# Degrees of the first graph: a search in the sorted destinations in place of a one-hot histogram, and the edge loads inside the first stage

## What is computed

```python
xn = _layernorm(x)
x = x + gnn(xn, (src, dst), w1, b1, gamma, beta, w2, b2, w_gcn, b_gcn) + mix(xn)
x = x + ffn(_layernorm(x), edge_index, ...)

def gnn(x, edge_index, ...):
    h = x @ w1.T + b1
    h = relu((h - mean(h, 0)) * rsqrt(var(h, 0) + eps) * gamma + beta)
    xw = (h @ w2.T + b2) @ w_gcn.T
    # src, dst get one loop edge per node
    deg = segment_sum(ones, dst, n)
    dinv = rsqrt(max(deg, 1))
    return segment_sum(xw[src] * (dinv[src] * dinv[dst])[:, None], dst, n) + b_gcn
```

## Time and profile before

| | |
|---|---|
| median of three executions | 5221.02 us |
| span of the profiled execution | 6013.1 us |
| instructions | 46816 |
| TensorE matmul busy | 4326.3 us (72%) |
| VectorE busy | 2806.5 us (47%) |
| GpSimd busy | 2975.4 us (49%) |
| ScalarE busy | 805.6 us (13%) |

### The profile page before, as it was taken

How to read it: one execution, slowest core, us unless ns; L and a number is a source line. 1 busy time by engine, 2 the same in 40 slices (tenths; PEclk the granted TensorE clock), 3 DMA queues, 4 the chain that set the end, 5 groups by cost and what they waited for, 6 DMA issues and landing times. The chain is left out here.

```text
span 6013.1 us, 46816 instructions
## 1 busy us (share of the span) xinstructions
PE 4326.3 (72%) x14757; PEld 2849.2 (47%) x14757; DVE 2806.5 (47%) x6018; ACT 805.6 (13%) x1519; POOL 2975.4 (49%) x2919
## 2 busy tenths in 40 slices
PE   5999777778779888778886545778687777630077
PEld 3776644444445555555554533445454444420045
DVE  5777466565556545666664621222222222232066
ACT  1111511222200000000000110112121111110022
POOL 0000266666666556677776024555545554466600
PEclk8666888888877788777777556888888888765589
DMA  3110533333344455333336552232223232232078
GB/s 102 48 53 30 145 112 112 113 112 113 107 113 132 141 137 144 91 90 90 90 90 79 177 147 50 81 89 84 69 74 88 83 87 80 60 85 54 11 180 220
DMA packets 257510, 596.30 MB, mean 99 GB/s; under 512 B 86189, under 2 KB 142304, under 8 KB 251903
## 3 DMA queue, kind: packets, MB, share of 16 engines
q0 software_dynamic: 119696, 294.84, 18.8%
q1 hardware_dynamic: 137582, 298.62, 17.9%
HBM read 437.77 MB, written 155.48 MB: 99 GB/s over the span
## 5 line engine op out<-in xcount | busy, mean ns | idle before, releaser
L941 POOL DMA_INDIRECT g_rows<-table,gcn_srcT x1664 | 1770.3, 1064 | 799.3 <-issue 472.8
L1804 POOL DMA_INDIRECT n_rows<-gtab,so_own x1122 | 1092.0, 973 | 885.2 <-DVEq L1923 551.2
L1011 PE MATMUL g_ps<-g_rows,g_hot 128*125 128x256 f32 x3328 | 1103.4, 472 | 225.5 <-issue 169.0
L1296 DVE TENSOR_TENSOR acc<-acc,g_ps 125x256 f32 x1664 | 697.3, 419 | 927.7 <-PE g_ps L1011 508.0
L1011 PEld LDWEIGHTS g_ps<-g_rows,g_hot 128*125 128x125 f32 x3328 | 723.1, 233 | 507.0 <-issue 342.9
L1750 PE MATMUL p_py<-f_w,f_hh 128*125 128x256 f32 x2688 | 678.8, 402 | 265.4 <-issue 261.9
L1744 PE MATMUL p_ph<-f_xfT,f_w 128*128 128x500 f32 x1344 | 627.7, 618 | 256.2 <-ACT f_hh L1975 128.5
L1750 PEld LDWEIGHTS p_py<-f_w,f_hh 128*125 128x125 f32 x2688 | 533.6, 199 | 426.8 <-issue 352.8
L1947 DVE TENSOR_TENSOR p_ob<-p_py,p_xb 125x512 f32<-125x512 f32 x168 | 114.7, 690 | 1299.9 <-remote 793.0
L1744 PEld LDWEIGHTS p_ph<-f_xfT,f_w 128*128 128x128 f32 x1344 | 268.8, 201 | 580.5 <-issue 433.2
L471 PE MATMUL a_pdeg<-so_x 125*100 125x125 bf16 x1600 | 372.5, 407 | 41.2 <-DVE so_x L552 41.2
(11 more groups left out here) (330 smaller groups left out, 4373.4 us busy)
## 6 DMA issues: line engine op xcount, KB each, us to landing
o_d<-p_ob SPq DMA_DIRECT2D x21, 1920.0 KB
z_ob<-o_d SPq DMA_DIRECT2D x21, 1920.0 KB
g_rows<-table,gcn_srcT POOLq DMA_INDIRECT x1664
n_rows<-gtab,so_own POOLq DMA_INDIRECT x1122
gout<-n_o SPq DMA_DIRECT2D x33, 408.0 KB
xnT_d<-a_xnT SPq DMA_DIRECT2D x25, 500.0 KB, 2.9
m_area<-xnT_d SPq DMA_DIRECT2D x25, 500.0 KB
qT_d<-m_area SPq DMA_DIRECT2D x25, 500.0 KB
```

Source lines behind the costliest of these rows:

```text
L941: pool.indirect_dma_start(out=rows[:, g % RING, j], out_offset=None, in_=K.table, in_offset=bass.IndirectOffsetOnAxis(ap=K.gcn_srcT[:, 4 * ...
L1011: mm = pe.matmul(ps[q, p % 4, b], hot[:, g % 4, 2 * j + b], rows[:, g % RING, 2 * j + b], start=True, stop=True, skip_group_check=True)
L1296: dve.tensor_tensor(a, a, ps[q, p % 4, b], ALU.add).then_inc(add_s, 1)
L1804: pool.indirect_dma_start(out=rows[:, c % 3, j], out_offset=None, in_=K.gtab, in_offset=bass.IndirectOffsetOnAxis(ap=K.gat_src[:, c * W + ...
```

## The change

The one-hot comparisons and the 1600 products are gone from `first_half`. For every tile t and partition p the kernel now finds how many edges have a destination below node 125 t + p, in two steps, and takes differences of neighbours for the degrees (126 partitions are used, so that each has its successor):

- The sorted destinations are written as 16-bit numbers into a DRAM table `gcn_dst` of 500 rows of 400. Every row's first value is spread over all partitions once (`phead`, 126x500 in PSUM, one product).
- Step one, `outside`, on VectorE: four comparisons per block of `phead` with the node number, each summed over its 500 columns. `choose` turns the counts into row numbers.
- GpSimd gathers those rows, four gathers of 126 rows of 800 bytes per block of nodes, into one of three buffers.
- Step two, `inside`, on ScalarE, three blocks later: four `Sign` activations of 126x400, each summed over its columns.
- Two small products at the end make degrees of the differences.

`load_edges` no longer exists. Its loads, the pair table, its write and the order check stand inside `first_half`, spread over the first blocks. What it did for unsorted edges alone moves behind the branch on the flag, in `places` and a new `degrees_unsorted`; so three branched stages now stand between `first_half` and `table_rows`, where two stood between `load_edges` and `first_half`.

```diff
-def load_edges(nc, m, K, A):
...
+def degrees_unsorted(nc, K):
...
+SPAN = 400
+HEADS = E_GCN // SPAN
+OWN = GCN_C // SPAN
+POST = TN + 1
...
             @block.sync
...
+                by_part = A.dst.rearrange("(p c) -> p c", p=c)
+                rows_in_two(sp, raw[:, 1], by_part, dst_s)
                 load(0)
                 for t, a in ((w1T, A.w1T), (w2, A.w2), (wgT, A.wgT)):
                     sp.dma_start(t[:], a.rearrange("(c p) o -> p c o", p=P)).then_inc(w_s, 16)
...
+                sp.wait_ge(short_s, 1)
+                rows_in_two(sp, K.gcn_dst.rearrange("(p i) h -> p (i h)", p=c), short, rows_out)
                 load(1)
                 load(2)
+                rows_in_two(sp, raw[:, 0], A.src.rearrange("(p c) -> p c", p=c), src_s)
 
                 sp.wait_ge(blank_s, 1)
...
+                    if k == 3:
+                        sp.wait_ge(pay_s, 2)
+                        rows_in_two(sp, K.gcn_pairs[0:E_GCN].rearrange("(p c) a -> p c a", p=c), K.gcn_pay, pairs_out)
...
+            @block.gpsimd
+            def _(pool):
...
+                pool.wait_ge(rows_out, 32)
+                for g in range(NB):
+                    pool.wait_ge(row_s, g + 1)
+                    if g >= DEEP:
+                        pool.wait_ge(side_s, 4 * (g - DEEP + 1))
+                    for j in range(4):
+                        pool.indirect_dma_start(out=rows[z, g % DEEP, j], out_offset=None, in_=K.gcn_dst,
+                                                in_offset=bass.IndirectOffsetOnAxis(ap=row[z, 4 * g + j:4 * g + j + 1], axis=0)
+                                                ).then_inc(got[g % DEEP], 16)
 
             @block.tensor
...
                 for k in range(NB):
-                    degrees(k * each)
+                    turn(k)
                     if k == 0:
                         pe.wait_ge(w_s, 16 * 5)
-                    turn(k)
-                    degrees(k * each + 1)
-                    degrees(k * each + 2)
                     project(k)
-                    degrees(k * each + 3)
...
+                pe.wait_ge(diff_s, 4)
+                pe.matmul(pdeg[q, 1, 0:NT], diff[z, 1], row_f[z], start=True, stop=False)
+                pe.matmul(pdeg[q, 1, 0:NT], diff[z, 0], inner[z], start=False, stop=True).then_inc(both_s, 1)
...
             @block.scalar
...
+                def inside(g):
+                    act.wait_ge(got[g % DEEP], 64 * (g // DEEP + 1))
...
+                    for j in range(4):
+                        t = 4 * g + j
+                        act.activation(seen[z, j], rows[z, g % DEEP, j], ACT.Sign, bias=minus[z, t:t + 1],
+                                       accum_out=side[z, t:t + 1]).then_inc(side_s, 1)
...
+                    if k in (1, 2):
+                        paired(2 - k)
+                    if k >= 3:
+                        inside(k - 3)
...
+                for g in range(NB - 3, NB):
+                    inside(g)
...
             @block.vector
...
+                def outside(g):
...
+                    for j in range(4):
+                        t = 4 * g + j
+                        dve.tensor_scalar(met[z, j], phead[z], node[z, t:t + 1], None, ALU.is_lt, ALU.add,
+                                          accum_out=heads[z, t:t + 1]).then_inc(met_s, 1)
...
                 for k in range(NB):
-                    if k:
-                        onehot(k * each)
                     if k + 1 < NB:
                         statistics(k + 1)
-                    onehot(k * each + 1)
+                    outside(k)
                     if k + 1 < NB:
                         normalise(k + 1)
-                    onehot(k * each + 2)
+                    choose(k)
                     if k:
                         of_h(k - 1)
-                    onehot(k * each + 3)
+                    check_order(k)
```

More of the change, by code:

```diff
@@ L305, in _ @@
                     scatter.run(pool, 0, GCN_C // ROUND)
-def load_edges(nc, m, K, A):
[L312 to L315, removed]
+def degrees_unsorted(nc, K):
+    HB = 16
+    rounds = GCN_C // HB
+    c = GCN_P
     with ExitStack() as ctx:
         m = Mem(nc, ctx)
[L319 to L330, removed]
-        with nc.Block() as block:
[L332 to L337, removed]
-                sp.wait_ge(copied, 2)
-                sp.dma_start(K.gcn_pairs[0:E_GCN].rearrange("(p c) a -> p c a", p=c), K.gcn_pay[0:c]).then_inc(out_s, 16)
-                sp.wait_ge(pad, 1)
-                sp.dma_start(K.gcn_pairs[E_GCN:E_GCN + P], tail[:]).then_inc(out_s, 16)
-                sp.wait_ge(out_s, 32)
-            @block.gpsimd
-            def _(pool):
-                pool.memset(tail[:, 0:1], 0).then_inc(chain, 1)
-                pool.memset(tail[:, 1:2], -1).then_inc(chain, 1)
-                pool.wait_ge(chain, 2)
-                pool.sem_inc(pad, 1)
@@ new lines, in degrees_unsorted @@
+        number = m.sb("du_number", [P, TN, HB], BF16)
+        on = m.sb("du_on", [P, TN, HB], BF16)
+        ot = m.sb("du_ot", [P, HB, NT], BF16)
+        blank = m.sb("du_blank", [P, P], BF16)
+        by_tile = m.sb("du_by_tile", [P, TN])
+        deg = m.sb("du_deg", [P, NT])
+        psum = m.ps("du_psum", [P, TN])
+        pturn = m.ps("du_pturn", [P, NT])
+        node_s, tile_s, used, numbered, deg_s, both_s, root_s = (m.sem("du_" + s) for s in (
+            "node", "tile", "used", "numbered", "deg", "both", "root"))
@@ L449, in _ @@
                         sp.dma_start(t[:], a.rearrange("(c p) -> p c", p=P)).then_inc(w_s, 16)
+                with nc.allow_non_contiguous_dma(reason="one value per partition"):
+                    sp.dma_start(after[0:c - 1], by_part[1:c, 0:1]).then_inc(after_s, 16)
+                sp.wait_ge(short_s, 1)
+                rows_in_two(sp, K.gcn_dst.rearrange("(p i) h -> p (i h)", p=c), short, rows_out)
                 load(1)
                 load(2)
+                rows_in_two(sp, raw[:, 0], A.src.rearrange("(p c) -> p c", p=c), src_s)
                 sp.wait_ge(blank_s, 1)
```

235 lines of the change are left out of this document (161 added, 74 removed).

## The result

| | before | after |
|---|---|---|
| median | 5220.52 us (5213.09 to 5234.57) | 4903.05 us (4898.74 to 4919.78), four executions |
| ratio | | 0.939, 95% interval 0.9368 to 0.9412 |
| first instruction of `table_rows` in the trace | 593.8 | 271.5 |

What follows compares the result with a forecast made beforehand. TensorE was taken to bound `first_half`. Opening 34 and loop 283 us gained, less 13 given back at the end, made 304, cut to 228 for the runs: 4990 us from 5221, range 4905 to 5060.

Steps and rivals of the forecast that it cites:

- From the profile to the runs: Step from profiled span 6013 to median 5221: old block taken at 17.2 us instead of 20.5, gain 228 instead of 304.
- The sum: Forecast gain in the profiled span, from opening, loop and end together: 304 us less.
- the stage unchanged by the recorder, 4917: Case that `first_half` is not affected by the span's excess, so the whole 304 us is gained: 4917 us, chance 0.1.
- Opening: Start of `first_half`: zeros issued at about 15 us instead of 49.4, block 3's statistics at 77 instead of 111.3, 34 gained.
- Loop: Blocks of nodes in `first_half`: 8.2 us each instead of 20.5, over 23 blocks, 283 us gained.
- End: After the last block: remaining `Sign` groups, differences and three branched stages before `table_rows`, giving back 13 us.
- Rival 1: In the runs VectorE, not TensorE, bounds the old loop at 16.3 us a block: 5014 us, chance 0.2.
- Rival 2: New loop stays slow: TensorE's clock stays low, 9.4 us a block, 5018, or DMA takes 10.2, 5036; chance 0.2.
- Rivals 3 and 4: Gathers at 6 us stall ScalarE: 5340 us, chance 0.03; unsorted stages run: nothing measurable, 0.02 shared with gain lost elsewhere.

Runs made afterwards that it cites:

- Experiment 1: The kernel before, unchanged, profiled a second time: 5219.5 us with a span of 5217.8.
- experiment 2: Kernel before with eight more histogram products per round, 800 in all, into PSUM that is not read: 5395.04 us, ratio 1.0362.
- experiment 6: Kernel after with VectorE's four comparisons made for the first block alone, counts copied for the others, degrees wrong: 4882.7 us, ratio 0.9353.
- experiment 7: Kernel after with `Sign` on ScalarE one block behind instead of three: 4912.72 us, ratio 0.9403 to the kernel before.
- experiment 8: Kernel after without the three branched stages between `first_half` and `table_rows`: 4892.41 us, ratio 0.9365 to the kernel before.
- experiment 11: Kernel after with zeros written in 25 pieces, one behind each block's store, and two of four comparisons moved to ScalarE: 4833.53 us, ratio 0.927.
- experiment 3: Kernel after with the write of zeros in two pieces, 120 and 5 partitions: 4882.38 us, ratio 0.9359 to the kernel before.
- experiment 5: Kernel before with its write of zeros cut into 120 and 5 partitions, nothing else: 5197.46 us, ratio 0.996.

## Why the prediction was wrong, and where it was right

- **The step that failed is "From the profile to the runs".** The sum came to 304 us, the trace gave 322 and the runs 317. The prediction then cut 304 to 228, on the guess that part of the 792 us of excess lay in the stage "with the most instructions per microsecond on TensorE". Experiment 1 and the stretches put 786 of the 792 in two later stages, and none in this one: what that step took for a share of this stage measured 0.5 us (550.6 against 550.1). Without that step the prediction would have been 5221 - 304 = 4917, 14 us off. The case it names for this ("the stage unchanged by the recorder, 4917") had a chance of 0.1 and was the one that came.
- **What the page of before already showed**: 793.0 us of idle time ended by "remote" on VectorE and 476.8 on ScalarE (L1975), both in a later stage. The prediction said that no view shows where the difference lies. The rows don't give its size, but they point away from `first_half`, in whose groups none stands.
- **Opening**: 34 forecast, 29.8 measured. The zeros' issue was right (15 against 15.30). The stuck time was not: the queue was free 61.9 us after the issue (77.15), where 57.6 had been carried over. The write now shares the queues with the other loads of the opening and with the first eight gathers; how much each of these adds was not tried.
- **Loop**: the parts were right, the total too careful. Comparison 0.66 against 0.658, `Sign` 0.6 against 0.61, gathers 1.25 against 1.30. The row sum for VectorE was 7.7 and the block took 7.30; the half microsecond added for in-order engines losing time to each other (8.2) never came: from block 3 to the last, VectorE waited for nobody. That is 23 x 0.9 = 21 us, the largest part of what the sum itself lacked.
- **End**: 13 given back forecast, 10.6 left over in the same count. The three groups of `Sign` took 8.4 us with a wait of 0.67 for the last gathers (7.5 forecast), the barriers 10.1 (11 forecast).
- **Rival 1**, chance 0.2: refuted by experiment 2. The prediction weighed the trace's 0.233 us for a weight load and product against the Trainium skill, page "TensorE: Matmul & The Clock Gate", section "Back-to-back issue gap", which gives about 81 ns. Runs without a profile say 0.228 (0.217 to 0.255 by the interval): the measurement decides against the page's figure for these pairs. Whether their operands' layout is the reason was not tried.
- **Rival 2**, chance 0.2: half seen. Mixed clock did occur (0.87 between 200 and 240), but it never stayed low. The two slowest projections, 6.50 and 6.66 us, put the next one 8.3 and 8.5 us behind them; the one after it was fast again and TensorE caught up, so VectorE never waited. From 84.8 us to the end of the loop every slow projection stands behind a wait of 2.2 us or more (not every such wait has one), and none behind a wait of 1.7 or less; in experiment 6, with waits of 0.95 us (one of 1.21) from 120 to 200 us, the clock stayed at 1.00. The section "HAM oscillation — how this bites in real kernels" of the Trainium skill's page "TensorE: Matmul & The Clock Gate" tells of bursts shorter than the waits between them, each of which starts at the low clock. The trace agrees with it where the wait was that long: the projection behind the opening's wait of 50.44 us took 6.17. In the loop its outcome, the low clock at every burst, did not come. The prediction left that condition out and so held the rule for this loop, whose waits are shorter than its bursts (2.8 against some 4.5).
- **Rivals 3 and 4**: the first gather of the group used at 243.54 is issued at 227.06, which leaves 16.5 us; experiment 7 shows that 7.4 do, but for one group that took 15.9. Between 261.4 and 271.4 us no engine ran anything of the branched stages' bodies; passing through the three still cost 6.0 us (experiment 8).

## What to carry to other kernels

When a profiled span is longer than the median, find the excess before scaling anything by it: look in every stage for idle time ended by a releaser that no engine of the kernel explains, and take another profile if one can be had. A term that was read from rows shouldn't be shrunk by a guess about another term. In a loop in which one engine has no wait in the trace, its own time is the period: 7.30 us here, for a row sum of 7.7 and of 5.3 to 7.3 for the others. Where two engines come within a tenth of each other (6.1 and 6.2 in experiment 11), the block took 6.4. Work moved ahead of a long transfer only uncovers the transfer: here cutting it up gave another 46 us, for a few lines.

## What the runs showed of the hardware

- While a write from 125 partitions was the traffic, 99 GB/s moved with a DMA share of 0.38 (kernel after, 40 to 60 us). With the write as 120 and 5 partitions, and other traffic beside it, it was 236 GB/s at a share of 1.00, where the uncut write had 155 at 0.61 (experiment 3, 16 to 40 us). In the old kernel the same cut was worth 16 us (experiment 5). The Trainium skill, page "DMA: Bandwidth & Descriptors", section "Why a DMA increments its semaphore by 16 and not by 1", says that a transfer is dealt to the largest number of engines up to 16 that divides its outer dimension. That would be 5 for 125 partitions and 15 for 120 (an estimate from the page's rule), shares of 0.31 and 0.94. The measured 0.38 and 1.00 agree in kind and lie a little above; the same view shows 1.07 for one stretch of the kernel after (10 to 16 us), so it reads somewhat high.
- A weight load and a product of 125 columns take 0.228 us in runs without a profile (experiment 2), and 0.233 in the trace, at either level of the clock.
- A comparison of 126x500 f32 in PSUM with a sum starts every 0.658 us on VectorE, a `Sign` of 126x400 16-bit numbers with a sum every 0.61 on ScalarE, one of 126x500 f32 every 0.70 (144.59 to 145.99 for two).
- Four gathers of 126 rows of 800 bytes are issued in 4.9 us. In the loop they had landed 2.0 us later; with the DMA share at 0.82 to 1.07 it was 10.5 us (experiment 7).
